# Two attention layers with routed experts between them: results scattered to token order, and two accumulating loads a group in place of eight gathers

## The chip, the cores and the metric

One core of one Trainium2 chip runs the whole program. The metric is the time of one execution on the device, in microseconds (us); the median of the runs of each kernel counts.

## The reference

The input x is 64 sequences of 128 tokens of 128 numbers (8192 tokens). Four layers follow each other, each added to its input:

```
x = x + L0_xattn(layernorm(x), side, ctx)     # 16 heads of 8; keys: 128 side rows and 120 ctx rows
x = x + L0_ffn(layernorm(x))                  # 8 experts, the best 2 for each token
x = x + L1_xattn(layernorm(x), ctx, ctx)      # 16 heads of 8; keys: 120 ctx rows
x = x + L1_ffn(layernorm(x))                  # 8 adapters of rank 64, the best 2 for each token
```

The part that the change touches is the second:

```
logits[t, e] = sum_j softmax_j(q[t, e] * k[t, j]) * v[t, j]        # q, k, v = x @ wqkv.T
top_logits, idx = top_k(logits, 2); scores = softmax(top_logits)
for each token t and each choice c: a, g = split(x[t] @ w1[idx[t, c]].T)
    out[t, c] = ((silu(a) * g) @ w2[idx[t, c]].T) * scores[t, c]   # silu(a)*g: 352 wide
combined[t] = out[t, 0] + out[t, 1]
```

## The kernel before

The 64 sequences are worked on in 16 groups of four (GB = 4). The program has five stages, each a block with its own instruction streams for the engines, and a barrier after each: constants, attention layer one with the router, the expert tiles, attention layer two, and the adapter layer.

**Attention layers** (`attention_layer`). Each engine runs `step(g)` for g = -4, -3, ...; step g holds work of several groups at once: x of group g+4 is loaded and prepared, group g+3 is normalised and turned, its k made and split into three bf16 parts, q of group g+2 is made and split, maxima of the scores are taken for g+1, scores, exponents and values are computed for g, and the output of g-1 is finished. PE goes through eight units (heads and sequences) a step, with lists `jobs` and `UNIT` that fix the place of every other job (XT turns the normalised x, QP and KP make q and k, VP the values, MT the maxima, OB, AT and OP the output). Every queue is in order, so a late job holds what stands behind it. Q and k parts go to DRAM scratch and come back as stacks (`write_q`, `write_k`, `load_q`, `load_k` on SP).

**Routing** (`Router`). In layer one, two steps behind, each token's two experts are picked, and a position within the expert's region of the DRAM tensor `routed_in` is counted out (`form_slots`, L1105). POOL scatters each normalised row, with its gate in column D, to this place (`scatter`, L1209): eight indirect DMAs a group of 128 rows each. SP fills 128 rows behind each expert's end with zeros (L293) and eight spare blocks as well (L289).

**Expert tiles** (`expert_tiles`, L1277). 135 tiles of 128 rows, in sequence. SP loads tile t+3 when its buffer is free, which is when DVE has written y of the tile six before (L1330). PE turns tile t+2, multiplies tile t+1 by the first weights (12 matmuls) and tile t by the second (6 passes). ACT and POOL copy the weights of the tile's expert to small buffers (L1391, L1344). DVE multiplies y by the gate (L1444) and POOL stores the 128 rows to `routed_out` in the order of the tiles (L1347). Because the tiles are packed, DVE works out at the stage's start where each token's two rows will stand (`slots_all`, L1417 to L1422).

**Layer two** adds the two expert results to x when it loads it: SP loads x of a group (L267), and POOL issues eight indirect DMAs, four sequences times two choices, each of which gathers 128 rows of `routed_out` and adds them to x (`gather`, L419). The second four wait for the first four. POOL's order in a step is: split q of g+2, gathers of choice 0 for g+4, split k of g+3, 1/deviation of g+3, gathers of choice 1 for g+4, residual and bias for g. DVE takes statistics of g+3 when the gathers have landed (L667).

Of the kernel before, what the change touches and what calls it, by code (L numbers as in the profile page):

```python
# [5 lines left out]
F32 = mybir.dt.float32  # L6
BF16 = mybir.dt.bfloat16
I32 = mybir.dt.int32
ACT = mybir.ActivationFunctionType
ALU = mybir.AluOpType  # L10
# [5 lines left out]
E = 8  # L16
# [68 lines left out]
def attention_layer(nc, x_in, x_out, side_t_in, ctx_in, ctx_t_in, layer, consts, route, stacks, ys=None, expert_w=None):  # L85
# [84 lines left out]
    with ExitStack() as c:  # L170
# [44 lines left out]
        if not first:  # L215
            gathered = [two(lambda p: sem(f"gathered{p}{k}")) for k in range(TOP)]
# [44 lines left out]
        def _(sp):  # L261
            def load_x(gl):
                q = gl.par
                emptied(sp, gl + -NX, "OP")
                if not first:
                    wait(sp, gathered[0][q], gl.pair * GB * 16)
                sp.dma_start(x_t[gl.n % NX][:], x_in[gl.n]).then_inc(x_loaded[q], 16)  # L267
# [21 lines left out]
            def zero_spare_rows():  # L289
                for k in range(E):  # L290
                    sp.dma_start(route.xs[SPARE + k * S:SPARE + (k + 1) * S], route.zeros[:]).then_inc(route.zeroed, 16)

            def zero_end_rows():  # L293
                sp.wait_ge(route.ends_ready, 1)
                for e in range(E):
                    row = sp.value_load(route.end_row[0:1, e:e + 1], min_val=e * REGION, max_val=e * REGION + TOKENS)
                    sp.dma_start(route.xs[bass.ds(row, S)], route.zeros[:]).then_inc(route.zeroed, 16)
# [102 lines left out]
        def _(pool):  # L400
# [18 lines left out]
            def gather(g4, first_one, last_one):  # L419

                if not g4.exists:
                    return
                if first_one == 0:
                    pool.wait_ge(x_loaded[g4.par], (g4.pair + 1) * 16)
                else:
                    pool.wait_ge(gathered[0][g4.par], (g4.pair + 1) * GB * 16)
                for b, k in [(b, k) for k in range(TOP) for b in range(GB)][first_one:last_one]:
                    nc.gpsimd.indirect_dma_start(  # L428
                        out=x_t[g4.n % NX][:, b], out_offset=None, in_=ys,
                        in_offset=bass.IndirectOffsetOnAxis(ap=route.slots_all[:, g4.n, b, k:k + 1], axis=0),  # L430
                        compute_op=ALU.add).then_inc(gathered[k][g4.par], 16)

            def step(g):
# [55 lines left out]
                else:  # L489
# [12 lines left out]
                    gather(g + 4, 0, GB)  # L502
# [6 lines left out]
                    gather(g + 4, GB, GB * TOP)  # L509
# [101 lines left out]
        def _(dve):  # L611
# [50 lines left out]
            def statistics(g3, part):  # L662
                if part == 0:
                    if first:
                        dve.wait_ge(x_loaded[g3.par], (g3.pair + 1) * 16)
                    else:
                        dve.wait_ge(gathered[1][g3.par], (g3.pair + 1) * GB * 16)  # L667
                    wait(dve, aggregated, g3.n)
# [234 lines left out]
def constants(nc, c, w_attn, b_attn, b_rows, wqkv_t, route):  # L903
# [7 lines left out]
    with ExitStack() as p:  # L911
# [12 lines left out]
        def _(pool):  # L924
# [17 lines left out]
            done(nc.gpsimd.tensor_copy(route.iota_t[:], route.iota_ti[:]))  # L942
            done(nc.gpsimd.memset(route.zeros[:], 0.0))

# [35 lines left out]
class Router:  # L980
# [124 lines left out]
    def form_slots(self, dve, g, part):  # L1105
# [16 lines left out]
        else:  # L1122
            self.after(dve, g, "slots")
            v.tensor_copy(self.xn[g.par][:, 0, :, D], self.g0[:])
            v.tensor_tensor(self.xn[g.par][:, 1, :, D], self.e2[:], self.g0[:], ALU.mult)
            v.tensor_copy(self.slot[g.par][:], self.slot_f[:]).then_inc(self.slot_ready, 1)
            v.tensor_copy(self.route.slots_f[:, bass.ds(g.n * (GB * TOP), GB * TOP)], self.slot_f[:].rearrange("s b k -> s (b k)"))
# [127 lines left out]
class Route:  # L1255


    def __init__(self, nc, c, xs):
# [5 lines left out]
        self.slots_f = sb("slots_f", [S, NG * GB * TOP])  # L1264
        self.count, self.region0 = sb("count", [S, E]), sb("region0", [S, E])
        self.iota_e, self.iota_ei = sb("iota_e", [S, E]), sb("iota_ei", [S, E], I32)
        self.slots_all = sb("slots_all", [S, NG, GB, TOP], mybir.dt.uint32)
        self.tile_row, self.tile_expert = sb("tile_row", [S, TILE_COLUMNS], I32), sb("tile_expert", [S, TILE_COLUMNS], I32)
        self.end_row, self.zeros = sb("end_row", [1, E], I32), sb("zeros", [S, ROW])
# [7 lines left out]
def expert_tiles(nc, ys, route, stacks):  # L1277
# [4 lines left out]
    with ExitStack() as c:  # L1282
# [18 lines left out]
        crossed, moved = sb("crossed", [S, NG * GB * TOP, E - 1]), sb("moved", [S, NG * GB * TOP])  # L1301
        order = sem("order")

# [20 lines left out]
        def _(sp):  # L1324
            sp.wait_ge(route.zeroed, 2 * E * 16)

            def step(t):
                tl = t + 3
                if has(tl):
                    wait(sp, y_ready, tl - NX + 1)  # L1330
# [5 lines left out]
        def _(pool):  # L1336
            pool.wait_ge(route.w2_loaded, 16)

            def step(t):
# [5 lines left out]
                if has(ts):  # L1345
                    pool.wait_ge(y_ready, ts + 1)
                    pool.dma_start(ys[ts * S:(ts + 1) * S], y_t[ts % NY][:]).then_inc(y_stored[ts % NY], 16)  # L1347
# [52 lines left out]
        def _(dve):  # L1400
            v = nc.vector
            region0, slots_f, slots_all = route.region0, route.slots_f, route.slots_all
            links = [0]

            def link(ins):
                links[0] += 1
                ins.then_inc(order, 1)
                dve.wait_ge(order, links[0])

            def prepare_stacks(k):  # L1410

                for rows, value in ((stacks.of_queries(0), 0), (stacks.of_keys(0, SC), ONE_ONE)):
# [3 lines left out]

            each = [S, NG * GB * TOP, E - 1]  # L1417
            link(v.tensor_tensor(crossed[:], slots_f[:].unsqueeze(2).to_broadcast(each),
                                 region0[:, 1:E].unsqueeze(1).to_broadcast(each), ALU.is_ge))
            link(v.tensor_tensor(crossed[:], crossed[:], route.delta[:, 0:E - 1].unsqueeze(1).to_broadcast(each), ALU.mult))  # L1420
            link(v.tensor_reduce(moved[:], crossed[:], AX.X, ALU.add))
            link(v.tensor_tensor(slots_all[:].rearrange("s n b k -> s (n b k)"), slots_f[:], moved[:], ALU.subtract))  # L1422
# [262 lines left out]
def encoder(nc, a, out):  # L1685
# [3 lines left out]
    ys = nc.dram_tensor("routed_out", (TILES * S, D), F32, kind="Internal").ap()  # L1689
# [51 lines left out]
```

## Time and profile before

| what | value |
|---|---|
| median of 3 runs | 1629.61 us (1625.89 to 1629.79) |
| span of the profiled execution, first to last instruction | 1619.5 us |
| PE / DVE / ACT / POOL busy | 83% / 70% / 54% / 61% |
| constants, then layer one | 0 to 4.8, then to about 685 us |
| expert tiles | about 685 to 983 us |
| layer two | about 983 to 1426 us |
| adapter layer | to 1619 us |
| POOL: gathers in layer two | 128, 200.9 us busy |
| POOL: stores in the expert stage | 135, 72.7 us busy |
| load of a group's x in layer two (256 KB), issue to landing | 4.4 us median |

The profiled execution's own time is not listed apart from its span; the median of the timed runs lies 10.1 us above the span, which is the program's start and end. A profile lists for each engine what it did and what ended its idle time; "issue" is idle time for which the profile shows no releaser. PEclk is the granted clock of TensorE, as a share of 2.4 GHz.

### The profile page before, as it was taken

The page shows a single profiled execution, that of the slowest core. Times are in us where ns is not written, and L with a number is a line of the kernel's source. Part 1 is how long each engine was busy: PE and PEld are TensorE (multiplying, and loading weights), DVE is VectorE, ACT ScalarE, POOL GpSimd, SP SyncE. Part 2 cuts the span into 40 slices and gives each one's busy share as a digit, 9 for nine tenths or more (in the row PEclk, how much of TensorE's full clock was granted, in tenths as well). Part 3 has the DMA queues.
Part 4 walks back from the last instruction along what each step waited for, and adds up shares of the span by engine and source line. Part 5 has one row for each costly group of instructions (what it writes and reads, how often), then busy time and mean ns, then how long its engine had stood idle before and what let it go on. Part 6 is the DMA issues. An engine that isn't in the chain of part 4 may idle for free. (4 is left out here: it accounts for less than half of the span.)

```text
span 1619.5 us, 46602 instructions
## 1 busy us (share of the span) xinstructions
PE 1352.2 (83%) x16805; PEld 1116.4 (69%) x16805; DVE 1128.8 (70%) x3395; ACT 873.4 (54%) x1634; POOL 984.3 (61%) x1122
## 2 busy tenths in 40 slices
PE   1689899898999988199999992369898889959999
PEld 0368677777777777199999991157676767747777
DVE  5779877787888885456555553368887888647776
ACT  1267666666766657066666660145565566624444
POOL 4447678777788866544444444888888886012221
PEclk9799999899999999599999995689999999969999
DMA  6667766666666642322222223678888787221221
GB/s 179 191 185 230 211 202 184 181 184 184 210 192 181 212 133 86 122 62 66 65 65 64 64 63 91 162 186 218 219 223 229 218 219 220 77 65 66 78 71 53
DMA packets 197816, 239.32 MB, mean 148 GB/s; under 512 B 39281, under 2 KB 165105, under 8 KB 190433
## 3 DMA queue, kind: packets, MB, share of 16 engines
q1 hardware_dynamic: 164608, 209.51, 42.5%
q0 software_dynamic: 26848, 25.91, 7.6%
q8 instruction: 131, 2.15, 0.6%
q10 hardware_dynamic: 6144, 1.06, 0.4%
q14 instruction: 85, 0.69, 0.1%
HBM read 148.34 MB, written 87.00 MB: 145 GB/s over the span
## 5 line engine op out<-in xcount | busy, mean ns | idle before, releaser
L701 DVE TENSOR_REDUCE L_neg_max<-L_ps_mx 128x2 f32<-128x496 f32 (+1 forms) x768 | 492.1, 659 | 140.0 <-PE L_ps_mx L851 136.5
L580 ACT ACTIVATE L_p<-L_ps_sc 120x512 f32<-120x512 f32 (+1 forms) x768 | 419.3, 598 | 228.3 <-PE L_ps_sc L838 225.7
L851 PE MATMUL L_ps_mx<-stack_k,stack_q 118*128 118x248 bf16 (+1 forms) x2048 | 303.3, 252 | 53.2 <-DMA stack_q<-L_q_rows 27.7
L838 PE MATMUL L_ps_sc<-stack_q,stack_k 122*120 122x128 bf16 (+1 forms) x3072 | 303.0, 223 | 6.1 <-DMA stack_q<-L_mT 4.7
L838 PEld LDWEIGHTS L_ps_sc<-stack_q,stack_k 122*120 122x120 bf16 (+1 forms) x3072 | 243.8, 124 | 69.0 <-issue 39.9
L428 POOL DMA_INDIRECT L_x<-routed_out,route_slots_all x128 | 200.9, 1570 | 49.0 <-issue 31.5
L871 PE MATMUL L_ps_o<-L_p,L_v 120*9 120x128 f32 (+1 forms) x6144 | 225.5, 281 | 3.3 <-ACT L_o_sb L607 2.7
L851 PEld LDWEIGHTS L_ps_mx<-stack_k,stack_q 118*128 118x128 bf16 x2048 | 149.7, 101 | 102.5 <-DVE L_neg_max L701 42.1
L871 PEld LDWEIGHTS L_ps_o<-L_p,L_v 120*9 120x9 f32 (+1 forms) x6144 | 145.8, 92 | 43.2 <-issue 25.3
L1436 DVE TENSOR_TENSOR M_hT<-M_act_a,M_ps_g 128x384 f32<-128x384 f32 x135 | 74.8, 554 | 126.3 <-ACT M_act_a L1396 120.4
L1344 POOL COPY M_w<-stack_q 128x384 f32 x135 | 69.1, 512 | 144.2 <-PE M_ps_y L1377 138.0
L1213 POOL DMA_INDIRECT routed_in<-R_xn,R_slot x128 | 127.0, 993 | 40.4 <-issue 32.2
L1391 ACT COPY M_w<-stack_k 128x768 f32 x135 | 112.1, 832 | 55.9 <-PE M_ps_g L1368 36.6
L1368 PE MATMUL M_ps_a<-M_xT,M_w 128*128 128x128 f32 x810 | 113.3, 276 | 0.0
L1368 PE MATMUL M_ps_g<-M_xT,M_w 128*128 128x128 f32 x810 | 113.1, 276 | 0.0
L1377 PE MATMUL M_ps_y<-M_w,M_hT 128*128 128x128 f32 x810 | 112.6, 275 | 0.0
L406 POOL TENSOR_TENSOR L_rem<-L_kf,L_k_parts_sb 128x512 f32<-128x512 f32 (+1 forms) x30 | 42.2, 1406 | 112.9 <-ACT L_k_parts_sb L545 94.1
L1396 ACT ACTIVATE M_act_a<-M_ps_a 128x384 f32<-128x384 f32 x135 | 66.2, 490 | 73.1 <-PE M_ps_a L1368 73.1
L1041 POOL TENSOR_SCALAR R_xn<-L_out,R_mv,R_rstd 128x128 f32<-128x128 f32 x120 | 94.2, 792 | 18.3 <-DMA routed_in<-R_xn,R_slot 17.8
L1368 PEld LDWEIGHTS M_ps_g<-M_xT,M_w 128*128 128x128 f32 x810 | 101.9, 193 | 0.0
L1368 PEld LDWEIGHTS M_ps_a<-M_xT,M_w 128*128 128x128 f32 x810 | 101.7, 193 | 0.3 <-DVE M_xT L1430 0.3
L1377 PEld LDWEIGHTS M_ps_y<-M_w,M_hT 128*128 128x128 f32 x810 | 101.3, 192 | 0.2 <-DVE M_hT L1436 0.2
(193 smaller groups left out, 2432.1 us busy)
## 6 DMA issues: line engine op xcount, KB each, us to landing
L_q_rows<-L_q_parts_sb SPq DMA_DIRECT2D x192, 192.0 KB
stack_q<-L_q_rows SPq DMA_DIRECT2D x192, 192.0 KB
stack_k<-L_k_rows SPq DMA_DIRECT2D x96, 372.0 KB
stack_k<-L_k_rows SPq DMA_DIRECT2D x96, 180.0 KB
L_k_rows<-L_k_parts_sb SPq DMA_DIRECT2D x32, 372.0 KB
M_x<-routed_in SPq DMA_DIRECT2D x135, 66.0 KB, 1.8
routed_out<-M_y POOLq DMA_DIRECT2D x135, 64.0 KB
x<-L_out SPq DMA_DIRECT2D x32, 256.0 KB, 3.6
```

Source lines behind the costliest of these rows:

```text
L428: nc.gpsimd.indirect_dma_start(out=x_t[g4.n % NX][:, b], out_offset=None, in_=ys, in_offset=bass.IndirectOffsetOnAxis(ap=route.slots_all[: ...
L580: nc.scalar.activation(p_t[t][u % 2][:, quarter * 4 * S:(quarter + 1) * 4 * S], ps_sc[n % NSC][0:KEYS[t], :], ACT.Exp).then_inc(sc_read, 1)
L701: nc.vector.tensor_reduce(neg_max[:, b, kk * HPB:(kk + 1) * HPB], v, AX.X, ALU.max, negate=True).then_inc(max_read, 1)
L838: last = mm(ps_sc[n % NSC][0:KEYS[t], j * S:(j + 1) * S], k_st[p][:, b // 2, h, b % 2, k0:k0 + KEYS[t]], q_st[p][:, b // 2, h, b % 2], sta ...
L851: last = mm(ps_mx[i % NMX][:, j * NK:(j + 1) * NK], q_st[p][0:TERM_TOP, b // 2, h, b % 2], k_st[p][0:TERM_TOP, b // 2, h, b % 2], start=Tr ...
L871: last = mm(ps_o[r:r + DH + 1, col:col + S], v_t[t][p][:, b, h, :], p_t[t][u % 2][:, j * S:(j + 1) * S], start=(t == 0), stop=(t == NT - 1))
L1041: last = vec.tensor_scalar(self.xn[g.par][:, k, b, 0:D], self.out_t[g.par][:, b], self.mv[:, b, 0:1], self.rstd[:, b:b + 1], ALU.subtract, ...
L1213: self.nc.gpsimd.indirect_dma_start(out=self.route.xs, out_offset=bass.IndirectOffsetOnAxis(ap=self.slot[g.par][:, b, k:k + 1], axis=0), i ...
L1368: last = nc.tensor.matmul(out[:, k * S:(k + 1) * S], w1[th % NW][:, half + k * 128:half + (k + 1) * 128], xT[p][:], start=True, stop=True)
L1377: last = nc.tensor.matmul(ps_y[p][:, 0:D], hT[p][:, k * S:(k + 1) * S], w2[ty % NW][:, k * D:(k + 1) * D], start=(k == 0), stop=(k == FC - 1))
L1391: nc.scalar.copy(w1[tw % NW][:], w1_all[:, bass.ds(e_w * W1, W1)]).then_inc(w1_ready, 1)
L1436: nc.vector.tensor_tensor(hT[p][:], act_a[p][:], ps_g[p][:, 0:FC * S], ALU.mult).then_inc(hT_ready, 1)
```

## The change

Each row that is scattered to `routed_in` now carries, beside its gate, a row number in column D+1: that of its token and choice in a new layout of `routed_out`, where for each group and each choice 512 rows stand in the order of the tokens. The zero rows carry numbers of spare rows. After an expert tile, POOL scatters y by that column, with an indirect DMA, instead of storing it by tile. The x buffer that holds the numbers is free only when the scatter has landed, so SP waits for that. The computation of `slots_all` on DVE is gone. Layer two adds choice 0 and choice 1 by one plain accumulating load each, of 128 partitions with 2 KB.

```
-            def gather(g4, first_one, last_one):
+            def add_routed(g4, k):
...
-                if first_one == 0:
+                if k == 0:
                     pool.wait_ge(x_loaded[g4.par], (g4.pair + 1) * 16)
                 else:
-                    pool.wait_ge(gathered[0][g4.par], (g4.pair + 1) * GB * 16)
-                for b, k in [(b, k) for k in range(TOP) for b in range(GB)][first_one:last_one]:
-                    nc.gpsimd.indirect_dma_start(
-                        out=x_t[g4.n % NX][:, b], out_offset=None, in_=ys,
-                        in_offset=bass.IndirectOffsetOnAxis(ap=route.slots_all[:, g4.n, b, k:k + 1], axis=0),
-                        compute_op=ALU.add).then_inc(gathered[k][g4.par], 16)
+                    pool.wait_ge(routed_added[0][g4.par], (g4.pair + 1) * 16)
+                rows = bass.ts(g4.n * TOP + k, S * GB)
+                pool.dma_start(x_t[g4.n % NX][:], ys[rows].rearrange("(s b) d -> s b d", b=GB),
+                               accum_op=ALU.add).then_inc(routed_added[k][g4.par], 16)
...
-                    gather(g + 4, 0, GB)
+                    add_routed(g + 4, 0)
...
-                    gather(g + 4, GB, GB * TOP)
+                    add_routed(g + 4, 1)
...
+            done(nc.gpsimd.iota(route.row_i[:], pattern=[[S * GB, TOP], [1, GB]], base=0, channel_multiplier=GB))
             done(nc.gpsimd.memset(route.zeros[:], 0.0))
+            done(nc.gpsimd.iota(route.zeros[:, :, D + 1].bitcast(I32), pattern=[[S, 2 * E]], base=TOKENS * TOP,
+                                channel_multiplier=1))
...
+            v.tensor_scalar(self.xn[g.par][:, :, :, D + 1].bitcast(I32), self.route.row_i[:], float(g.n * TOP * GB * S),
+                            None, ALU.add)
             v.tensor_copy(self.slot[g.par][:], self.slot_f[:]).then_inc(self.slot_ready, 1)
-            v.tensor_copy(self.route.slots_f[:, bass.ds(g.n * (GB * TOP), GB * TOP)], self.slot_f[:].rearrange("s b k -> s (b k)"))
...
-        self.end_row, self.zeros = sb("end_row", [1, E], I32), sb("zeros", [S, ROW])
+        self.end_row, self.zeros = sb("end_row", [1, E], I32), sb("zeros", [S, 2 * E, ROW])
...
-                    wait(sp, y_ready, tl - NX + 1)
+                    if has(tl - NX):
+                        sp.wait_ge(y_stored[(tl - NX) % NY], ((tl - NX) // NY + 1) * 16)
                     r = row_of(sp, tl)
...
-                    pool.dma_start(ys[ts * S:(ts + 1) * S], y_t[ts % NY][:]).then_inc(y_stored[ts % NY], 16)
+                    token_row = x_t[ts % NX][:, D + 1:D + 2].bitcast(mybir.dt.uint32)
+                    nc.gpsimd.indirect_dma_start(
+                        out=ys, out_offset=bass.IndirectOffsetOnAxis(ap=token_row, axis=0),
+                        in_=y_t[ts % NY][:], in_offset=None).then_inc(y_stored[ts % NY], 16)
...
-            each = [S, NG * GB * TOP, E - 1]
-            link(v.tensor_tensor(crossed[:], slots_f[:].unsqueeze(2).to_broadcast(each),
-                                 region0[:, 1:E].unsqueeze(1).to_broadcast(each), ALU.is_ge))
-            link(v.tensor_tensor(crossed[:], crossed[:], route.delta[:, 0:E - 1].unsqueeze(1).to_broadcast(each), ALU.mult))
-            link(v.tensor_reduce(moved[:], crossed[:], AX.X, ALU.add))
-            link(v.tensor_tensor(slots_all[:].rearrange("s n b k -> s (n b k)"), slots_f[:], moved[:], ALU.subtract))
...
-    ys = nc.dram_tensor("routed_out", (TILES * S, D), F32, kind="Internal").ap()
+    ys = nc.dram_tensor("routed_out", (TOKENS * TOP + 2 * E * S, D), F32, kind="Internal").ap()
```

## Rows read from the trace of the kernel before

**Rows 1.** Stretches: us; busy us (count) of PE, PEld, DVE, ACT, POOL; clock, DMA, GB/s.
```profile
700.00:980.00 280.00, 277.45 (x2486) 277.06 (x2484) 149.47 (x424) 170.55 (x259) 136.41 (x262) 1.00 0.23 64
1107.70:1341.40 233.70, 202.99 (x3013) 161.26 (x3011) 201.29 (x438) 135.79 (x260) 205.27 (x169) 0.96 0.83 222
1341.40:1363.00 21.60, 20.57 (x314) 16.65 (x314) 17.86 (x48) 13.48 (x27) 15.78 (x14) 1.00 0.68 191
```
**Rows 2.** Waits, 1090 to 1345 us: who waited for whom, total us, times, longest.
```profile
POOL L_x L428 <- issue: 20.8, 71, 0.3
```
**Rows 3.** Order of time, POOL: start us, us, instruction, [idle before, releaser].
```profile
1212.60 1.55 POOL L428 DMA_INDIRECT L_x<-routed_out,route_slots_all  x1 [0.30 <-issue]
```
**Rows 4.** Order of time, DVE's copies of xnT: groups 0, 2, 4, 14, 15.
```profile
1011.65 0.69 DVE L637 COPY L_xnT<-L_misc 128x512 f32<-128x512 f32 x1 [1.21 <-PE L_misc L798]
...
1062.28 0.69 DVE L637 COPY L_xnT<-L_misc 128x512 f32<-128x512 f32 x1
...
1108.80 0.68 DVE L637 COPY L_xnT<-L_misc 128x512 f32<-128x512 f32 x1
...
1343.53 0.68 DVE L637 COPY L_xnT<-L_misc 128x512 f32<-128x512 f32 x1
...
1364.03 0.68 DVE L637 COPY L_xnT<-L_misc 128x512 f32<-128x512 f32 x1
```
**Rows 5.** Line 709: times, ns minimum/median/maximum; 1050 to 1345, then from 1348.
```profile
L709 DVE CAST L_m_parts<-L_neg_max x25: 180/252/3524, 1050.9 to 1334.8; 128x32 bf16<-128x32 f32 x25
...
L709 DVE CAST L_m_parts<-L_neg_max x6: 180/181/181, 1357.0 to 1402.4; 128x32 bf16<-128x32 f32 x6
```
**Rows 6.** DMA queue, 1107.7 to 1341.4: packets, MB, share of 16 engines.
```profile
q0 software_dynamic: 11509, 5.24, 19.1%
```
**Rows 7.** Order of time: layer two's filling, and a stall in its steady part.
```profile
986.24 1.70 POOL L428 DMA_INDIRECT L_x<-routed_out,route_slots_all  x1 [7.54 <-DMA L_x<-x]
...
1006.28 0.87 DVE L671 BATCH_NORM_STATS2 L_stats<-L_x 128x6 f32<-128x128 f32 x4 [12.14 <-DMA L_x<-routed_out,route_slots_all]
...
1042.55 1.01 PE L851 MATMUL L_ps_mx<-stack_k,stack_q 118*128 118x120 bf16 x8
...
1247.86 0.63 PE L798 MATMUL L_misc<-C_ident,L_xn 128*128 128x128 f32 x4 [4.10 <-DVE L_xn L685]
```
**Rows 8.** Order of time, expert stage: one tile's y, transposition, w2 copy, store.
```profile
799.90 0.83 PE L1377 MATMUL M_ps_y<-M_w,M_hT 128*128 128x128 f32 x6
...
800.46 0.14 PEld L1360 LDWEIGHTS M_ps_x<-C_ident,M_x 128*128 128x128 f32 x1
...
800.90 0.51 POOL L1344 COPY M_w<-stack_q 128x384 f32 x1 [1.07 <-PE M_ps_y L1377]
...
801.42 0.54 POOL L1347 DMA_DIRECT2D routed_out<-M_y  x1
...
966.06 0.35 DVE L1444 TENSOR_SCALAR M_y<-M_ps_y,M_x 128x128 f32<-128x128 f32 x1
```
**Rows 9.** Layer one's scatters, line 1213; landings in 669 to 684, then 188 to 640.
```profile
634.31 1.09 POOL L1213 DMA_INDIRECT routed_in<-R_xn,R_slot  x1 [0.18 <-issue]
...
DMA to landing us min/median/max: 2.3/2.3/2.3
...
DMA to landing us min/median/max: 2.3/3.4/6.2
```
**Rows 10.** Line 1332, SP's loads, 690 to 980, with landings; line 1321, POOL's register load.
```profile
L1332 SPq DMA_DIRECT2D M_x<-routed_in x131: 337/338/347, 690.7 to 967.2; - x131
...
DMA to landing us min/median/max: 1.7/1.8/2.7
...
L1321 POOLq TENSOR_LOAD <-route_tile_expert x135: 285/296/511, 685.5 to 970.9; - x135
```
**Rows 11.** Order of time: two memsets on POOL.
```profile
3.71 0.21 POOL L943 MEMSET route_zeros<- 128x132 f32 x1
...
4.93 6.71 POOL L416 MEMSET stack_k<- 122x7936 int32 x1
```

More of the change, by code:

```diff
@@ L215, in attention_layer @@
         if not first:
-            gathered = [two(lambda p: sem(f"gathered{p}{k}")) for k in range(TOP)]
+            routed_added = [two(lambda p: sem(f"routed_added{p}{k}")) for k in range(TOP)]
         k_written = sem("k_written")
@@ L265, in load_x @@
                 if not first:
-                    wait(sp, gathered[0][q], gl.pair * GB * 16)
+                    wait(sp, routed_added[0][q], gl.pair * 16)
                 sp.dma_start(x_t[gl.n % NX][:], x_in[gl.n]).then_inc(x_loaded[q], 16)
@@ L290, in zero_spare_rows @@
                 for k in range(E):
-                    sp.dma_start(route.xs[SPARE + k * S:SPARE + (k + 1) * S], route.zeros[:]).then_inc(route.zeroed, 16)
+                    sp.dma_start(route.xs[SPARE + k * S:SPARE + (k + 1) * S], route.zeros[:, E + k]).then_inc(route.zeroed, 16)
             def zero_end_rows():
@@ L296, in zero_end_rows @@
                     row = sp.value_load(route.end_row[0:1, e:e + 1], min_val=e * REGION, max_val=e * REGION + TOKENS)
-                    sp.dma_start(route.xs[bass.ds(row, S)], route.zeros[:]).then_inc(route.zeroed, 16)
+                    sp.dma_start(route.xs[bass.ds(row, S)], route.zeros[:, e]).then_inc(route.zeroed, 16)
             def step(g):
@@ L666, in statistics @@
                     else:
-                        dve.wait_ge(gathered[1][g3.par], (g3.pair + 1) * GB * 16)
+                        dve.wait_ge(routed_added[1][g3.par], (g3.pair + 1) * 16)
                     wait(dve, aggregated, g3.n)
@@ L1263, in __init__ @@
         self.xs = xs
-        self.slots_f = sb("slots_f", [S, NG * GB * TOP])
         self.count, self.region0 = sb("count", [S, E]), sb("region0", [S, E])
         self.iota_e, self.iota_ei = sb("iota_e", [S, E]), sb("iota_ei", [S, E], I32)
-        self.slots_all = sb("slots_all", [S, NG, GB, TOP], mybir.dt.uint32)
+        self.row_i = sb("row_i", [S, TOP, GB], I32)
         self.tile_row, self.tile_expert = sb("tile_row", [S, TILE_COLUMNS], I32), sb("tile_expert", [S, TILE_COLUMNS], I32)
-        self.end_row, self.zeros = sb("end_row", [1, E], I32), sb("zeros", [S, ROW])
+        self.end_row, self.zeros = sb("end_row", [1, E], I32), sb("zeros", [S, 2 * E, ROW])
         self.iota_t, self.iota_ti = sb("iota_t", [S, TILE_COLUMNS]), sb("iota_ti", [S, TILE_COLUMNS], I32)
@@ L1299, in expert_tiles @@
         ps_a, ps_g = two(lambda p: pb(f"ps_a{p}", [128, 512])), two(lambda p: pb(f"ps_g{p}", [128, 512]))
-        crossed, moved = sb("crossed", [S, NG * GB * TOP, E - 1]), sb("moved", [S, NG * GB * TOP])
-        order = sem("order")
         x_loaded = [sem(f"x_loaded{i}") for i in range(NX)]
@@ L1401, in _ @@
             v = nc.vector
[L1402 to L1408, printed above, removed]
             def prepare_stacks(k):
```

## The prediction

> **What bounds the kernel now.** I read the busy shares by stretch first, then the waits, then the order of time. The page's 83% PE and 61% POOL hide stages with different limits. The stretches separate them [rows 1]: in the expert stage (700 to 980 us) PE is busy 277.45 of 280 us; in layer two's steady part (1107.7 to 1341.4) PE has 202.99, DVE 201.29 and POOL 205.27 of 233.70; after the last gather (1341.4 to 1363) PE has 20.57 of 21.60.
>
> Three engines at 87% look like a draw. The waits decide it: between 1090 and 1345 us POOL's longest wait is 20.8 us for "issue", 0.3 us before each of 71 gathers, and nearly nothing is another engine's [rows 2]. A gather is 1.55 us busy behind a gap of 0.30 [rows 3], so eight are 14.8 us a group. The copies of xnT, one a group, give the pace: 1108.80 to 1343.53 is ten groups at 23.47 us; with 20.53 us busy and 2.4 of gaps a group, POOL fills that. The next group, with no gather beside it, takes 20.50 [rows 4]. That row is the heart of my forecast.
>
> The gathers do a second harm. A tiny DVE cast (128x32) takes a median of 252 ns and up to 3.5 us in layer two while gathers run; after the last gather it takes 181 [rows 5]. The Trainium skill ("SBUF — State Buffer", Who interferes with whom) says that DVE and GpSimd share a pair of SBUF ports and the later to issue is blocked; by that rule these delays go with the gathers, and the row after the last gather agrees.
>
> **Layer two, steady part.** Removed: eight gathers, 14.8 us of POOL a group. Added: two accumulating loads of 256 KB. No row shows one. Lower end: POOL's plain store of 128 pieces, 0.54 us [rows 8]; upper end: rows of 2 KB prepared as four gathers' worth, 4 x 1.55 = 6.2 us. I take 0.9: the store is the nearest row, and an accumulating gather costs 1.55 against 1.0 for a plain scatter [rows 3, 9]. With gaps POOL then needs 8.7 + 2 x 1.2 = 11 us a group; at the upper end 8.7 + 12.4 = 21.1. The second load waits on POOL for the first to land, with the k split and the deviation (some 5 us) issued between them; a plain load of that size lands in 4.4 us here (table). If POOL waits a few us more, the residual addition and the next q split stand behind it, both with some 9 us in hand.
>
> Next in line is PE: 20.3 us busy a group at a mean granted clock of 0.96, and in the stretch without gathers 20.50 us a group at 1.00 [rows 1, 4]. PE's clock falls behind its stalls, such as 4.1 us for DVE's xn, which itself waits for POOL's late rstd [rows 7]; they go with their cause. I take 20.7 us a group: 10 x (23.47 - 20.7) = 27.7 us less. DMA: its engines are busy 0.83 of 23.47 = 19.5 us a group, of which 19.1% (4.5 us) is the software queue's [rows 1, 6]. The same bytes in a quarter of the pieces cost 1.1 us (by pieces) to 4.5 (by bytes): 16.1 to 19.5 us in 20.7, that is 78 to 94%. At that end DMA could hold a group near 22.
>
> **Layer two, filling.** Now the first group's eight gathers start at 986.24 and its statistics at 1006.28 [rows 7]. With two loads of about 3.7 us each behind x's landing at 986.2, x is ready at 993.8. So the first xnT copy moves from 1011.65 [rows 4] to 999.9, 12 us. Group 1: loads issued at 997.4 and 1001.2, landed at 1004.8; its keys leave PE two jobs after q of group 0, at about 1005.7, POOL splits them in 3.4 us and makes the deviation in 1.4: xnT at 1013.3. Group 2: the max tiles of group 0 can start at 1016 instead of 1042.55 [rows 7] and take DVE some 15 us: xnT at 1031.5 instead of 1062.28, 31 us. Then two groups to 1108.80, 46.5 us now [rows 4], at 21.3 each (their q stacks arrive barely in time): 3.9 more. Filling: 35 us less, between 25 (if only half of group 1's and 2's gain stays) and 38. From xnT of the last group on nothing changes.
>
> **Expert stage.** 135 tiles at 2.12 us, PE without a gap [rows 1]. Two parts change.
> The store becomes a scatter: POOL's instruction grows from 0.54 to 1.09 us, with a gap of 0.18 before it [rows 8, 9]. POOL needs 0.51 + 0.18 + 1.09 = 1.78 of 2.12 us. Its register load for the next tile (0.30 us, 0.5 with its checks [rows 10]) now runs in its sequencer beside the engine's work; if it ran only after the scatter, 2.26 us would be 0.14 over: 135 x 0.14 = 19 us, the upper end. I take 0.
> The x buffer now stays taken until the scatter has landed. The chain, from the end of y's matmuls of tile T-6 (799.90 + 0.83 = 800.73, call it 0) to the transposition of tile T: the w2 copy starts at 0.17 and ends at 0.68 [rows 8]; the scatter starts at 0.86 and is seen landed 2.3 to 2.45 us later [rows 9], at 3.3; SP's register load and issue take 0.8 (y at 966.06 + 0.35 = 966.41 [rows 8], the load's issue at 967.2 [rows 10]), the landing 1.8 [rows 10]: 5.9. PE wants it at 800.46 + 3 x 2.12 = 806.82 [rows 8], which is 6.09. The cover is 0.2 us. What goes over costs a quarter of itself a tile (y of T-2 follows the transposition of T in PE's order, so four tiles close the loop). Loads land in 1.7 to 2.7 us [rows 10], so a few tiles will stall: I take 4 us, between 0 and the 29 us of a landing of 3.4, the median under layer one's traffic [rows 9]: (1.1 - 0.2) / 4 x 129.
> The Trainium skill ("DMA: Bandwidth & Descriptors", Anatomy of one DMA) warns that the completion of a write to HBM can take surprisingly long. By it this edit alone could turn the change's sign; the third rival prices that.
> The route slots' four DVE instructions go from the stage's start, where they delay the first xT copy by less than 1 us; the last scatter lands less than 1 us later than the last store. I set the one against the other.
>
> **Layer one and constants.** A memset grows from 132 to 2112 elements a row: 0.21 us at 132, 6.71 at 7936 [rows 11], so 0.83 ns an element and 1.65 us more; two iotas with their waits, some 0.4. The barrier behind makes all later work 2.1 us late; nothing covers it. In form_slots one 128x8 operation replaces another. SP's zero rows keep their count and size.
>
> **Sum** against the profiled span of 1619.5: -27.7 - 35 + 4 + 2.1 = -56.6, so 1562.9. The runs' median is 10.1 us above the span (the program's start and end), so 1573.
>
> **Rivals.**
> A second bound holds layer two near 22 us a group: DMA at 94%, q stacks that come late, or loads that cost POOL 6 us. For it: DMA's 0.83. Against: 20.50 measured. The steady part saves 14.7, not 27.7, and the filling 3 less: 1573 + 16 = 1589.
> The expert stage grows by 20 to 28 us, not 4, because landings take 3.4 us or POOL's register load runs behind the scatter: about 1593. For it: 0.2 us of cover. Against: 2.3 us in all landings of the quiet stretch [rows 9], and DMA at 0.23 here [rows 1].
> The other side: the scatter's write takes as long as layer one's slowest landing, 6.2 us [rows 9]. Excess 3.9 - 0.2 = 3.7, a quarter a tile: 129 x 0.93 = 119, so 1573 - 4 + 119 = 1688, slower. It decides from about 60 us, an excess of 1.9, a landing of 4.4 us.
> The loads relieve POOL of nothing, because they are cut up finer than I bound: at 7.4 us each, POOL is where it was, and only part of the filling stays, about 1615. Against: no row with a price near that.
>
> **How the numbers follow.** Forecast 0.66; group near 22 us 0.15; expert stage longer by 20 to 28 us 0.13; slow landings 0.04, slower than before; loads at POOL's old price 0.02. The likeliest's own range is 1558 to 1586 (20.4 to 21.5 us a group, expert stage 0 to 10, filling 30 to 38). The range reaches from 1556 to 1602, over both middle rivals. A measurement of this kernel tells 0.3%, 5 us, from no change: faster 0.94, same 0.02, slower 0.04.
>
> **What would show it.** Right: xnT copies 20.4 to 21.2 us apart; POOL near 11 us busy a group and waiting for others; granted clock 0.98 or more; the 128x32 cast near 0.2 us; first statistics near 994 plus the 2 of the constants; expert tiles still 2.12 us apart. Wrong: PE waiting for M_x in tile after tile; POOL's M_w copies no longer waiting for PE; groups at 22 us or more with PE waiting for stack_q; an accumulating load over 3 us on POOL.

## The result, and the profile after

The changed kernel takes 1581.05 us, the median of five runs (1561.26 to 1587.28), against 1629.38 for the kernel before: a ratio of 0.967, 95% interval 0.963 to 0.971. The forecast was 1573. Ratios and intervals leave out runs more than 1.5% above the fastest of the same kernel (here the one of 1587.28 us). The profiled execution is the shortest of the five, 1561.26 us with a span of 1559.6; the other four lie at 1580 and above. Its stages are compared here with the profiled execution of before, so the stage differences below (59.9 us in all) are larger than the difference of the medians (48.3).

The stretches after, in the columns of [rows 1]: first the expert stage, from its first to its last scatter, then ten groups of layer two's steady part.

```profile
690.00:984.00 294.00, 287.09 (x2528) 284.04 (x2526) 152.72 (x431) 173.38 (x263) 197.29 (x267) 0.99 0.23 61
1082.00:1285.50 203.50, 195.31 (x3027) 155.80 (x3024) 167.44 (x442) 135.97 (x261) 100.36 (x110) 1.00 0.89 258
```

POOL's 205.27 of 233.70 us became 100.36 of 203.50 and the granted clock rose from 0.96 to 1.00. The copies of xnT, groups 0, 2, 4 and 14, answer to [rows 4]:

```profile
1007.04 0.69 DVE L635 COPY L_xnT<-L_misc 128x512 f32<-128x512 f32 x1 [1.21 <-PE L_misc L796]
...
1039.81 0.68 DVE L635 COPY L_xnT<-L_misc 128x512 f32<-128x512 f32 x1
...
1082.12 0.68 DVE L635 COPY L_xnT<-L_misc 128x512 f32<-128x512 f32 x1
...
1285.45 0.68 DVE L635 COPY L_xnT<-L_misc 128x512 f32<-128x512 f32 x1
```

Ten groups take 203.33 us, 20.33 each. What POOL now does, by order of time: the first three loads of the filling, with x's statistics, answering to [rows 7]; then, from the grouping by line, all 20 of the steady part (busy us, mean ns).

```profile
992.27 0.96 POOL L428 DMA_DIRECT2D L_x<-routed_out  x1 [7.44 <-DMA L_x<-x]
...
996.58 0.88 POOL L428 DMA_DIRECT2D L_x<-routed_out  x1 [3.34 <-DMA L_x<-routed_out]
...
1001.93 0.87 DVE L669 BATCH_NORM_STATS2 L_stats<-L_x 128x6 f32<-128x128 f32 x4 [1.65 <-DMA L_x<-routed_out]
```
```profile
L428 POOL DMA_DIRECT2D L_x<-routed_out x20 | 18.1, 903 | 0.0
```

A load costs POOL 0.90 us, and x is complete 5.35 us after the second load's start. The waits of the steady part: POOL, which waited for its own issue 71 times [rows 2], now waits for ScalarE, and TensorE's longest waits are for the stack of queries (1082 to 1285.5 us; total, times, longest).

```profile
POOL L_rem L406 <- ACT L_q_parts_sb L538: 84.2, 10, 8.7
...
PEld L_ps_sc L836 <- DMA stack_q<-L_mT: 17.0, 13, 2.6
```

The expert stage paid. Waits of its middle part, 700 to 985 us:

```profile
POOL M_w L1343 <- PE M_ps_y L1379: 66.7, 124, 3.5
...
PEld M_ps_x L1362 <- DMA M_x<-routed_in: 8.2, 13, 2.7
```

The trace of before has no row like the second one in this stretch. From first to last store the stage took 282.7 us; it now takes 293.5. TensorE's transpositions in order of time show where (start, duration, [idle before, releaser]): 2.12 us apart, except where a tile of x is late.

```profile
702.06 0.27 PE L1362 MATMUL M_ps_x<-C_ident,M_x 128*128 128x128 f32 x1
...
705.63 0.33 PE L1362 MATMUL M_ps_x<-C_ident,M_x 128*128 128x128 f32 x1 [1.29 <-DMA M_x<-routed_in]
...
707.81 0.27 PE L1362 MATMUL M_ps_x<-C_ident,M_x 128*128 128x128 f32 x1
```

The stages by their ends, before against after:
```
first store of the expert stage    695.47 -> 690.33    -5.1
first to last store                282.7  -> 293.5    +10.9
last store to layer two's x load     5.1  ->   5.5     +0.4
x load to xnT(4)                   125.6  ->  92.8    -32.8
xnT(4) to xnT(14)                  234.7  -> 203.3    -31.4
xnT(14) to the end                 276.0  -> 274.1     -1.9
```
The sum is -59.9, and the spans differ by as much (differences are taken before rounding). The first line holds the constants' +2.07 (layer one's first x load is issued at 6.88 instead of 4.81 us), so layer one itself came out 7 us shorter. No step of the change explains that; profiled executions of other kernels, with this layer one or the one before, put the first store anywhere from 690.1 to 699.9 us, and in the first set of experiments from 748.2 to 756.6.

### The profile page after: what moved, and what is told of

The parts are those of the page before. It is cut to its first block and busy times, and to the rows that moved or that the text cites. A ratio compares the mean times of both kernels' runs of the same rounds, so it can differ in the third digit from the quotient of the medians.

```text
span 1559.6 us, 46503 instructions
## 1 busy us (share of the span) xinstructions
PE 1345.3 (86%) x16805; PEld 1109.0 (71%) x16805; DVE 1091.0 (70%) x3391; ACT 872.2 (56%) x1634; POOL 871.8 (56%) x1028
## 5 line engine op out<-in xcount | busy, mean ns | idle before, releaser
L836 PEld LDWEIGHTS L_ps_sc<-stack_q,stack_k 122*120 122x120 bf16 (+1 forms) x3072 | 240.5, 123 | 71.8 <-issue 35.0
L869 PEld LDWEIGHTS L_ps_o<-L_p,L_v 120*9 120x9 f32 (+1 forms) x6144 | 145.3, 91 | 43.0 <-issue 25.5
L1347 POOL DMA_INDIRECT routed_out<-M_y,M_x x135 | 132.1, 978 | 28.1 <-issue 18.9
L406 POOL TENSOR_TENSOR L_rem<-L_qf,L_q_parts_sb 128x512 f32<-128x512 f32 x30 | 34.8, 1159 | 134.5 <-ACT L_q_parts_sb L538 134.5
```

The costliest lines, as they stand in the source:

```text
L836: last = mm(ps_sc[n % NSC][0:KEYS[t], j * S:(j + 1) * S], k_st[p][:, b // 2, h, b % 2, k0:k0 + KEYS[t]], q_st[p][:, b // 2, h, b % 2], sta ...
L869: last = mm(ps_o[r:r + DH + 1, col:col + S], v_t[t][p][:, b, h, :], p_t[t][u % 2][:, j * S:(j + 1) * S], start=(t == 0), stop=(t == NT - 1))
L1347: nc.gpsimd.indirect_dma_start(out=ys, out_offset=bass.IndirectOffsetOnAxis(ap=token_row, axis=0), in_=y_t[ts % NY][:], in_offset=None).th ...
```

## The experiments

The runs fall into three sets, the first two on one chip and the third on another. Each ratio is to the kernel before as it ran in the same set.

**The change repeated, and three parts of it** (before 1686.1 us here, 11 runs; the first store came some 50 to 65 us later in every profiled kernel, so ratios and stages count, not times).

*again*: the changed kernel, no edit.

> The changed kernel once more, because its runs lie 20 us apart (1561 to 1581). In the one trace the expert stage takes 293.6 us from the first to the last scatter against 282.7 of the stores before. Theory one: the expert stage carries the spread, because the x loads wait for the scatter's landing with 0.2 us of cover; a run near 1580 shows an expert stage of 305 us or more, with PE waiting for M_x in many tiles, and layer two at 20.3 us a group as in the first trace. Rival: the spread is in layer one or two; then the expert stage is 293 us again and the copies of xnT lie further apart.

1632.3 us, 0.969 (0.966 to 0.972). Expert stage 306.8 us, group 20.21. The gain repeats; the expert stage's loss was 24 us here, not 11. The time from a scatter's start to the issue of the load that waits for it was longer in this trace: a median of 3.43 us, against 3.00 in the first trace of the changed kernel. Waits, 760 to 1055 us:

```profile
PEld M_ps_x L1362 <- DMA M_x<-routed_in: 20.5, 29, 2.2
```

*nx9*: more buffers for x in the expert stage.
```diff
-        NX, NY, NW, PIECES = 6, 4, 3, 16
+        NX, NY, NW, PIECES = 9, 4, 3, 16
```

> Nine x buffers in the expert stage instead of six; loads still go three tiles ahead, so a load waits for the scatter nine tiles back, 6.4 us more of cover. Theory one (the loads wait for the landing): PE no longer waits for M_x, scatters 2.12 us apart, 283 us from first to last, and the time falls by 10 to 30 us against the changed kernel and its spread shrinks to a few us: 1548 to 1556. Rival (the scatter itself costs, by POOL's instruction or by its writes in DMA): the stage stays at 293 us or more and the time at 1561 to 1581.

1612.7 us, 0.957 (0.954 to 0.960). Expert stage 282.8 us, to 0.1 what it was before the change, with the scatter in place and with the same 3.4 us from its start to the load's issue as in *again*. So the whole loss comes through the x buffer that stays taken. The scatter's busy time on POOL costs nothing as occupancy; as a part of the time for which the buffer is held it still counts (see *plain_wait*).

*plain_store*: the old store by tile, which frees x at y_ready; the loads of layer two then add other tokens' rows, with the same addresses and sizes.
```diff
-                    if has(tl - NX):
-                        sp.wait_ge(y_stored[(tl - NX) % NY], ((tl - NX) // NY + 1) * 16)
+                    wait(sp, y_ready, tl - NX + 1)
...
-                    nc.gpsimd.indirect_dma_start(
...
+                    pool.dma_start(ys[ts * S:(ts + 1) * S], y_t[ts % NY][:]).then_inc(y_stored[ts % NY], 16)
```

> The expert stage as before (y stored by tile, x buffer free once y is written), layer two with the two accumulating loads; so the rows that are added are those of other tokens. Both theories: expert stage 282.7 us, layer two at 20.3 us a group: 1548 to 1556. If it is faster than nine buffers by more than 3 us, the scatter costs by itself and not only by the wait; if equal, only the wait did. If it still spreads by 20 us, the spread is not the expert stage's.

1613.9 us, 0.957 (0.954 to 0.960), expert stage 282.7 us: the same place as nx9 by the other road.

*g8*: the two loads undone. Eight accumulating gathers again, from the token-ordered rows, by row numbers made once by an iota.
```diff
-                rows = bass.ts(g4.n * TOP + k, S * GB)
-                pool.dma_start(x_t[g4.n % NX][:], ys[rows].rearrange("(s b) d -> s b d", b=GB),
-                               accum_op=ALU.add).then_inc(routed_added[k][g4.par], 16)
...
+                for b in range(GB):
+                    nc.gpsimd.indirect_dma_start(
+                        out=x_t[g4.n % NX][:, b], out_offset=None, in_=ys[0:TOKENS * TOP],
+                        in_offset=bass.IndirectOffsetOnAxis(ap=route.slots_all[:, g4.n, b, k:k + 1], axis=0),
+                        compute_op=ALU.add).then_inc(routed_added[k][g4.par], 16)
```

> The changed kernel with eight accumulating gathers a group again, from the rows in token order. Expert stage and constants are the change's, layer two's POOL work is that of before. Theory (POOL's gathers bound layer two): groups 23.4 us apart, POOL with no waits for others, the 128x32 cast up to 3.5 us, and the time is that of the changed kernel plus 60 to 75 us, that is 1630 to 1650, slower than before by what the expert stage and the constants cost. Rival (the order of the rows in memory makes layer two fast, not the number of POOL's instructions): groups under 22 us apart, under 1600.

1712.5 us, 1.017 (1.014 to 1.021), and 80 us above *again*, where 60 to 75 were expected. A group is 24.62 us, a little over before's 23.47 to 23.83 in two traces; the order of the rows in memory alone gives nothing, and the gain is that of the two large transfers. The stretch of ten groups:

```profile
1184.80:1431.00 246.20, 211.34 (x3024) 167.34 (x3022) 193.21 (x441) 136.99 (x261) 210.50 (x172) 0.92 0.79 211
```

**How the buffer loss scales, and half of the gathers** (before 1630.5 us, 17 runs).

*nx5*: `NX, NY, NW, PIECES = 5, 4, 3, 16`.

> Five x buffers in the expert stage instead of six. If the chain of the prediction is right (5.9 us from the end of y's matmuls to the landed load, then 2.4 us of PE's work to the next y, over a loop that is now three tiles long), a tile takes (5.9 + 2.4) / 3 = 2.76 us and the stage from the first to the last scatter 134 x 2.76 = 370 us; the time is 60 to 75 us above that of six buffers. Rival (the wait costs only where DMA is disturbed, the chain being shorter than worked out): under 320 us, and less than 20 us above six buffers.

1642.6 us, 1.009 (1.006 to 1.012). Expert stage 372.1 us. With five buffers the chain of 5.9 us has 6.09 - 2.12 = 3.97 to run in, and 98 of the 134 gaps between TensorE's transpositions are over 2.22 us. Waits, 700 to 1060 us:

```profile
PEld M_ps_x L1362 <- DMA M_x<-routed_in: 81.4, 89, 4.1
```

*nx7*: `NX, NY, NW, PIECES = 7, 4, 3, 16`.

> Seven x buffers: 2.1 us more of cover than six, so 2.3 us. In the trace of the repeated run stalls of up to 1.5 us, and a few of 2, follow 5 to 6 us after each instruction fetch of 16 KB. If disturbances of that size are the loss, nearly all of it goes: stage of 283 to 286 us, time within 4 us of nine buffers and 15 to 25 us below six. Rival (the landing is late by more, or POOL's scatter is the pace): stage over 290 us.

**1553.3 us, 0.954 (0.950 to 0.957)**. Expert stage 283.5 us. One buffer more, 2.12 us of cover, takes nearly all. Waits, 700 to 975 us:

```profile
PEld M_ps_x L1362 <- DMA M_x<-routed_in: 0.7, 1, 0.7
```

*plain_wait*: six buffers, the old store, but x's buffer is held until the store has landed: *plain_store* with the changed kernel's wait on SP. Layer two's added rows are again other tokens'.

> Six buffers and the wait for the store's landing as in the changed kernel, but the store is the plain one by tile (the rows that are added later are those of other tokens). It takes POOL 0.54 us instead of 0.98 and needs no gap before it, so the cover grows from 0.2 to about 0.8 us if both land equally fast after the instruction ends. Theory one (the wait for the landing is what costs, whatever is stored): stalls remain behind instruction fetches, stage 288 to 298 us. Rival (rows spread over memory land late): 283 to 285 us, as without the wait.

1560.2 us, 0.958 (0.953 to 0.962), expert stage 295.1 us; 26 gaps between transpositions are over 2.22 us, 12.3 us in all above 2.12. So a plain store that is waited for stalls the stage too, and the scattered rows are not the cause. How long the wait lasts does matter: from the store's start to the load's issue it is 2.60 us, not 3.00, and the median stands 7 us above that of *nx7*, while the changed kernel's ratios (0.964 to 0.969) stand 0.010 to 0.015, some 17 to 25 us, above it. The profiled execution of *plain_wait* is one of the slower of its six (1566.8 us), so its 295.1 us says less than the median.

*g4*: choice 0 by one load, choice 1 by four accumulating gathers, issued where the change issues its second load (behind the deviation).

> The changed kernel with choice 0 added by one accumulating load and choice 1 by four accumulating gathers from the token order. POOL needs 11 - 1.2 + 4 x 1.85 = 17.2 us a group, less than PE's 20.3. If POOL's occupancy alone was layer two's bound, groups stay 20.4 us apart, and the time is that of the changed kernel plus 5 us of filling. If the gathers also hold DVE's small operations back and PE behind them, groups are 21 to 22.5 us apart, the 128x32 cast takes up to 3.5 us, and the time is 15 to 35 us above the changed kernel.

1589.0 us, 0.977 (0.973 to 0.981). A group takes 19.94 us with POOL half as busy again as in the change:

```profile
1095.10:1294.50 199.40, 194.56 (x3024) 155.71 (x3022) 167.13 (x441) 134.68 (x261) 155.42 (x141) 1.00 0.93 261
```

So four gathers cost a group nothing, in this place; ten groups of the kernels with two loads took from 200.7 to 205.6 us. The whole kernel is slower than the changed one all the same, 0.977 against 0.964 to 0.969. Its filling is 4 us longer (97.2 us from layer two's x load to xnT(4)); the rest was not traced: the median of its seven runs lies 21 us above its profiled run of 1568.5, whose expert stage took 302.4 us.

**The best kernel, and the place of the gathers** (before 1626.6 us, 17 runs).

*best*: seven buffers, and the zeros cleared by VectorE.
```diff
-            done(nc.gpsimd.memset(route.zeros[:], 0.0))
+            pool.wait_ge(blank, 1)
...
+            nc.vector.memset(route.zeros[:], 0.0).then_inc(blank, 1)
...
-        NX, NY, NW, PIECES = 6, 4, 3, 16
+        NX, NY, NW, PIECES = 7, 4, 3, 16
```

> The changed kernel with seven x buffers in the expert stage, and the memset of the zeros on VectorE in place of GpSimd. Theory: the memset (1.86 us on GpSimd, 128x2112) held back GpSimd's issue of layer one's first work, so the constants end about 1.8 us earlier and layer one's first x load lands near 5.1 us from the span's start, not 6.9; the expert stage takes 283.5 us from first to last scatter as with seven buffers alone, a group of layer two 20.3 us; 0.953 of the kernel before. Rival: VectorE needs the same time for it and layer one's start waits for that; then the start stays and the time is that of seven buffers alone.

**1554.2 us, 0.953 (0.950 to 0.957)**, expert stage 283.4. The x load moves only from 6.88 to 6.25, 0.6 us instead of 1.8: the memset takes 1.82 us on VectorE too, and POOL's first iota starts only behind its end, at 3.43 instead of 2.17 (the rival's outcome in the main; what makes the iota late was not tried). 0.6 us is less than the time can tell: *nx7* and *best* are equal (0.954 and 0.953).

```profile
1.31 1.82 DVE L948 MEMSET route_zeros<- 128x2112 f32 x1 [1.31 <-PEq L1720]
...
3.43 0.14 POOL L935 IOTA route_iota_ei<- 128x8 int32 x1
...
5.18 0.16 POOL L943 IOTA route_zeros<- 128x16 int32 x1
...
6.25 0.33 SPq L267 DMA_DIRECT2D L_x<-in_x  x1
```

*g4_early*: the same four gathers and one load as g4, in the other order: gathers ahead of the split of the keys, the load behind the deviation.

> Choice 0 of each token by four accumulating gathers issued where the change issues its first load (ahead of the second half of the group's routing), choice 1 by one accumulating load. Theory (occupancy): GpSimd has room for four gathers wherever they stand, a group takes 20 to 20.5 us, VectorE's 128x32 casts stay near 0.2 us in the mean. Rival (position): gathers at this place lie beside VectorE's casts and delay rstd; casts are stretched to up to 3.5 us, TensorE waits for xn, and a group takes 21 us or more, 10 us or more over the stage.

1653.9 us, 1.015 (1.010 to 1.019): 1.5% slower than before the change, where *g4* was 2.3% faster, by the place of four gathers and one load. Ten groups take 255.3 us, 25.5 each, while POOL's busy time is that of g4:

```profile
1123.60:1378.90 255.30, 212.14 (x3017) 170.51 (x3015) 184.66 (x441) 132.93 (x260) 156.94 (x141) 0.90 0.75 205
```

One group of it by order of time, POOL, then VectorE and TensorE:

```profile
1207.68 1.16 POOL L406 TENSOR_TENSOR L_rem<-L_qf,L_q_parts_sb 128x512 f32<-128x512 f32 x1 [7.52 <-ACT L_q_parts_sb L543]
...
1210.92 1.66 POOL L431 DMA_INDIRECT L_x<-routed_out,route_slots_all  x1 [0.16 <-issue]
...
1216.58 1.54 POOL L431 DMA_INDIRECT L_x<-routed_out,route_slots_all  x1 [0.30 <-issue]
1217.56 1.70 POOL L406 TENSOR_TENSOR L_rem<-L_kf,L_k_parts_sb 128x480 f32<-128x480 f32 x1
...
1221.38 1.05 POOL L498 TENSOR_TENSOR L_rstd<-L_rstd,C_half_neg 128x4 f32<-128x4 f32 x1
1222.39 0.98 POOL L426 DMA_DIRECT2D L_x<-routed_out  x1
1223.07 1.60 POOL L517 TENSOR_TENSOR L_x<-L_x,C_bias_bc 128x512 f32<-128x512 f32 x1
```
```profile
1222.46 2.57 DVE L688 TENSOR_SCALAR L_xn<-L_x,L_mv,L_rstd 128x128 f32<-128x128 f32 x2 [2.70 <-POOL L_rstd L498]
...
1226.74 1.09 PE L801 MATMUL L_misc<-C_ident,L_xn 128*128 128x128 f32 x4 [4.73 <-DVE L_xn L688]
```

POOL stands idle 7.5 us for ScalarE and is then late with rstd, because 7.2 us of gathers lie between the split of q and it. VectorE waits 2.7 us for rstd; its first two normalisations then take 2.57 us (the first of them 2.31), where two take 0.60 in the change: POOL's load and residual addition run beside them, and the first one ends 0.1 us after the addition. TensorE waits 4.73 us for xn, and its mean granted clock over the ten groups is 0.90. The chain xnT, q, split, gathers, split, deviation, xn closes on itself at 25.5 us. VectorE's 128x32 casts, which the rival expected stretched to 3.5 us, stay at 0.23 in the mean.

*again2*: the changed kernel a third time.

> The changed kernel once more, on the chip of the two others. Theory: the excess of the expert stage over 2.12 us a tile is 11 to 27 us by the run, each stall behind a late load of an x tile into one of six buffers; 0.967 to 0.970 of the kernel before, and slower than seven buffers by 0.013 to 0.015. Rival: the loss belongs to the first two chips alone and the ratio comes to 0.955.

1572.6 us, 0.964 (0.961 to 0.967). Expert stage 305.5 us; 29 gaps between transpositions are over 2.22 us, 22.4 us in all above 2.12. It is slower than *best* by 18 us (0.0105, where 0.013 to 0.015 was expected), and the two profiled expert stages differ by 22. Waits, 760 to 1003 us:

```profile
PEld M_ps_x L1362 <- DMA M_x<-routed_in: 17.0, 21, 2.5
```

*before_again*: the kernel before, with a profile.

> The kernel before itself: a group of layer two 23.4 to 23.5 us, expert stage 282 to 283 us from first to last store, ratio 1.00. It shows how far layer one's length and the filling differ between profiled executions of one kernel.

1631.1 us, 1.001 (0.997 to 1.005). Expert stage 282.7 us, ten groups 238.3 us (23.8 each, forecast 23.4 to 23.5), first store 695.6.

## Why the prediction was nearly right, step by step

**Layer two, steady part: right, by a larger sum.** 31.4 us less where 27.7 were taken. POOL's price of a load was 0.90 against 0.9, a group 20.33 against 20.7, the clock 1.00. The row of the group without a gather [rows 4], 20.50, was the better guide; the 0.2 added to it was not needed. DMA's share came out at 0.89, inside the 78 to 94% given, and did not hold a group; *g4* ran at 0.93 and 19.94 us. TensorE is now the busiest engine by far: 195.31 of 203.50 us.

**But its reason was too simple.** The prediction let POOL's busy time, 20.5 of 23.47 us, set the pace. If occupancy were all, *g4* and *g4_early*, both with 15.6 us of POOL a group, would be equal. One takes 19.94 and the other 25.5. What parts them is a chain through rstd (the 1/deviation). Its three legs, as means over the ten groups:

```
us                                   before    g8   g4_early  after    g4
copy of xnT to POOL's split of q        4.5    5.2       5.8    3.9   4.0
split of q to the end of rstd          15.0   15.1      14.8    9.7   9.3
end of rstd to the next copy of xnT     4.0    4.4       5.0    6.7   6.7
of it, until VectorE starts xn          0.7    1.1       0.0    3.4   3.3
```

With gathers ahead of the deviation the middle leg is 15 us and rstd comes with next to nothing in hand; without them it is 9.7, and rstd is there 3.4 us before VectorE asks for it. The kernel before has the same four gathers in that place and still runs at 23.47, so these do not make the 25.5 alone: the other 2 us are the two outer legs, with the normalisations held up beside the load and the addition and TensorE at a lower clock. In the kernel before POOL is fully occupied as well, so there the two readings do not part. The late rstd was named [rows 7] but only as what a stall does to the clock.

The second harm, the stretched casts [rows 5], was also worth more than the prediction made of it. Over the ten groups the 128x32 cast takes a median of 572 ns in before and 276 in *g8*, up to 3.5 and 3.6 us, and 181 in all 20 of the change. TensorE's longest waits in before are for what these casts lead to, 1.7 us of the 3.1 a group for which it was idle (L812 turns what the casts made); in *g4_early*, where the casts stay short, they are for xn. Waits, before from 1107.7 to 1341.4 us, then *g4_early* from 1123.6 to 1378.9:

```profile
PEld L_misc L812 <- issue: 21.5, 20, 3.5
PE L_misc L812 <- DVE L_m_parts L711: 16.9, 6, 3.2
```
```profile
PE L_misc L801 <- DVE L_xn L688: 43.2, 10, 4.8
```

No run takes the casts' delay away and leaves POOL full, so how much of before's 23.47 us each of the two made is open.

**Filling: right.** 32.8 us less against 35. The loads land 4.3 and 5.3 us after they start, not in 3.7 each. Counted from layer two's x load, the first xnT copy comes 10.8 us earlier where 12 were taken, and the third 28.6 where 31 were; the missing 2 are there.

**Constants: right.** 2.07 against 2.1.

**Expert stage: the step that failed.** 4 us were taken, 10.9 measured, and 24.1 and 22.8 in the two other profiled executions. So the cost of the buffer's wait was mis-sized. The rival with 20 to 28 us had the size of the two later executions, but neither of its causes holds. The register load does not run behind the scatter (*nx9*: 282.8 us with the scatter in place), and there is no landing of 3.4 us in every tile: in the first trace the load is issued 3.00 us (median) after the scatter's start, the landing and SP's own 0.7 included. The failed sentence is "What goes over costs a quarter of itself a tile". It suits a chain that is late throughout, as in *nx5*: 370 expected from the same chain, 372.1 measured. It is wrong for single late tiles. There TensorE, busy all of its 2.12 us, has nothing to catch up with, and each costs all that goes over the cover. The second half of the mistake is that medians were put into a chain with so little cover, and the question was only whether the mean went over. Put together again from the trace after (0.84 to the scatter's start, 3.00 to the load's issue, 1.8 for its landing), the chain is 5.6 us and the cover 0.4; in *again*, with 3.43 us, it is next to nothing. The trace after shows one case in full (POOL's scatter, then TensorE's transposition):

```profile
937.78 0.98 POOL L1347 DMA_INDIRECT routed_out<-M_y,M_x  x1 [2.84 <-DVE M_y L1432]
```
```profile
943.17 0.33 PE L1362 MATMUL M_ps_x<-C_ident,M_x 128*128 128x128 f32 x1 [2.55 <-DMA M_x<-routed_in]
```

The usual gap is 0.16; this one is 2.68 longer. TensorE waits 2.55 for it 5.4 us later. The kernel before has the same gap in the same place, harmless there:

```profile
937.60 0.54 POOL L1347 DMA_DIRECT2D routed_out<-M_y  x1 [2.68 <-DVE M_y L1444]
```

So the cover could have been tested against the longest gap of before's own expert stage rather than its median; that would have found this one stall of the 11 us. The other stalls of this trace, 0.1 to 1.6 us, fit single late landings, but it has no landings of these transfers. The trace of *plain_wait* has them for two thirds of the loads and a quarter of the stores: x's load took 1.7 to 3.7 us with a median of 1.8, the store 1.8 to 3.5 with a median of 1.8, and nine late tiles there have a load of 2.9 us or more. By gaps of over 2.22 us between transpositions the changed kernel has 17 late tiles in one execution, 33 and 29 in two others, and before has one. The load was issued over 3.3 us after the scatter's start in 19 of 129 tiles of the first, 108 and 40 of the others.

**The sum.** By the spans it was -56.6 forecast and -59.9 measured. Layer two's steady part gave 3.7 more, the filling 2.2 less, the expert stage lost 6.9 more, and layer one was 7.2 shorter, which no step of the change explains. That last one is luck: without it the spans would differ by 52.7.

The step from the span to the time was wrong. The prediction and the table before it took 10.1 us for the program's start and end. In every run on record that lists both, the time is 1.7 to 1.8 us above the span of the same execution (1561.26 and 1559.6 in the result). The profiled execution of before, with its span of 1619.5, was thus one of some 1621 us, faster than all five timed ones, and the other 8 us were the spread between executions. After the change the median lies 21 us above the profiled span. So the span came out 3 us below the forecast and the median 8 us above it. The ratio's three values, 0.967, 0.969 and 0.964, are 51 to 59 us of 1630 less, against 56.6 forecast: the size was right, with a gain of layer two that was under-forecast, a loss of the expert stage that was under-forecast too, and 7 us of luck in the one trace.

**Open.** Why the number of late tiles differs between executions. A part of it goes with the instruction queue, which moves 16 KB at a time, 22 times in the stage. In *again* 19 transpositions are over 0.4 us late, and 14 of them start 2 to 3 us after the start of such a transfer (14.7 of the 23.0 us); the gap between the scatters follows 5 to 6 us after it. In *again2* it is 10 of 15 (12.5 of 22.4 us), in the first trace only 2 of 8, with as many transfers. Of all tiles, late or not, one in eight starts 2 to 3 us after one. That is a correlation; no run changed the instruction stream. Also open is what holds POOL for 2.7 us ahead of the 114th store, in each of seven traces looked at for it, before's too; why layer one's length moves by 10 us between executions; and the 20 us between the first profiled run and its four neighbours, of which a longer expert stage would explain 12. No run tried the *g4* order with seven buffers; its groups are within what kernels with two loads show, and its filling is 4 us longer, so little can be expected of it.

## What to carry to other kernels

When a change lets a buffer be held until a DMA has landed, compare the loop's chain with its cover at the longest gap of the trace, not at the median; here one buffer more, a change of one number, brought 18 us and more where the cover was a few tenths of a us. A term of "lateness per tile over the tiles in the loop" holds for steady lateness alone; single events count nearly in full on an engine that is busy throughout. And a span is compared with the span of one execution, not with a median: look how far the two lie apart for the same execution. Last, ask of a busy engine not only how many microseconds it has but what stands ahead of the one result that others wait for: with the four gathers behind such a result and the load ahead of it a group took 5.6 us less than with the two exchanged.

## What the runs showed of the hardware

- An accumulating plain load of 256 KB costs POOL 0.88 to 1.24 us (median 0.91 of the 32 in layer two) and lands 4.0 to 5.8 us after its start (median 5.1); four accumulating gathers of the same bytes cost 7.4 with their gaps (4 x 1.55 and 4 x 0.30).
- A scatter of 128 rows of 512 B costs POOL 0.95 to 0.99 us in the expert stage, not layer one's 1.09 in the row that was read.
- VectorE's normalisation of two 128x128 blocks, 0.60 us, took 2.57 beside POOL's load and 128x512 addition in *g4_early*; over ten groups the mean of one block went from 340 to 723 ns. The Trainium skill ("SBUF — State Buffer", Who interferes with whom) says that where an instruction of VectorE uses both pairs of ports, the later of it and GpSimd to issue is blocked until the other ends. The rows agree in part: VectorE started 0.07 us behind the load's start and was held, but until the end of the addition, which had started after it.
- A 128x32 cast of VectorE, 0.18 us alone, took up to 3.5 us in before while POOL ran gathers and additions back to back.
- DMA engines at a mean share of 0.93 did not slow a group of layer two (19.94 us in *g4*).
